# Cross-attention on one core: ScalarE writes the rounded keys to both of their places, instead of one write and a transfer on chip

## What is computed

```python
q = x @ Wq + 2 * (x @ Aq @ Bq)          # 16 x 112 x 1024 -> 32 heads of 32
k = ctx @ Wk + 2 * (ctx @ Ak @ Bk)      # 16 x 375 x 1024 -> 8 heads of 32
v = ctx @ Wv + 2 * (ctx @ Av @ Bv)
scores = einsum('bhqd,bhtd->bhqt', q, k) / sqrt(32)
attn = softmax(scores, axis=-1)
out = x + lora_linear(attn @ v, Wo, Ao, Bo)
```

## Time and profile before

| | us |
|---|---|
| median of 3 runs | 974.63 |
| lowest and highest | 973.23, 975.2 |
| the profiled execution's own time | 971.95 |
| its span, first to last instruction | 969.9 |
| PE busy | 939.5 (97%) |
| VectorE busy | 578.4 (60%) |
| ScalarE busy | 431.7 (45%) |
| GpSimd busy | 320.3 (33%) |

### The profile page before, as it was taken

One profiled execution on the slowest core, in us unless ns is written; L12 is line 12 of the kernel. 1 busy time (PEld: TensorE's weight loads), 2 busy tenths in 40 slices (PEclk: granted clock), 3 DMA queues, 4 the chain that ended last, 5 costly groups with the idle time before them and its releaser, 6 DMA issues.

```text
span 969.9 us, 15636 instructions
## 1 busy us (share of the span) xinstructions
PE 939.5 (97%) x5904; PEld 796.3 (82%) x5904; DVE 578.4 (60%) x1005; ACT 431.7 (45%) x843; POOL 320.3 (33%) x276
## 2 busy tenths in 40 slices
PE   6989999989899999999999999999999989999998
PEld 4879998988878878878888888887887867688886
DVE  5764424246776876776876876876876862343331
ACT  3432313132465665665665665665665644410010
POOL 1300000300244543653553553554454454500000
PEclk9999999999999999999999999999999999999999
DMA  6657597672334534526526526517517364486632
GB/s 197 202 165 197 210 262 268 217 204 66 80 91 108 120 82 117 142 69 152 140 56 165 139 50 172 129 53 174 126 40 184 89 228 125 151 248 207 197 131 87
DMA packets 112794, 141.60 MB, mean 146 GB/s; under 512 B 30688, under 2 KB 90208, under 8 KB 112720
## 3 DMA queue, kind: packets, MB, share of 16 engines
q1 hardware_dynamic: 109552, 129.07, 48.8%
q10 hardware_dynamic: 3168, 11.54, 3.2%
HBM read 95.98 MB, written 38.21 MB: 138 GB/s over the span
## 4 chain that ended last, share of the span: by engine, by line
PE 87%; DVE 5%; DMA 4%; ACT 2%; issue 1%; SPq 1%; POOL 0%; DVEq 0%; POOLq 0%
PE ps L770 13%; PE ps L771 13%; PE ps L772 13%; PE ps L965 9%; PE ps L949 8%; PE ps L980 8%; PE ps L912 5%; PE ps L914 5%; PE ps L916 5%; PE ps L855 4%; PE ps L1016 2%; DMA wo_scratch<-w_sum_qkv 2%; DMA q_scratch<-q_out_lo 1%; PE ps L810 1%; DVE w_sum_qkv L1220 1%
## 5 line engine op out<-in xcount | busy, mean ns | idle before, releaser
L1334 DVE TENSOR_REDUCE maxima<-ps 112x1 f32<-112x375 f32 x512 | 268.4, 542 | 72.1 <-PE ps L965 65.8
L1142 ACT ACTIVATE probs<-ps 125x448 f32<-125x448 f32 x384 | 208.7, 544 | 159.1 <-PE ps L949 157.8
L752 POOL TENSOR_TENSOR prob_sum<-probs 125x448 f32<-125x448 f32 x128 | 148.8, 1178 | 327.3 <-ACT probs L1142 327.0
L965 PE MATMUL ps<-k_stack,q_stack 96*112 96x376 f32 x512 | 177.0, 346 | 5.8 <-DVE maxima L1334 3.0
L758 POOL TENSOR_TENSOR prob_sum<-prob_sum,probs 125x448 f32<-125x448 f32 x128 | 145.4, 1151 | 16.9 <-ACT probs L1142 15.0
L949 PE MATMUL ps<-q_stack,k_stack 97*125 97x448 f32 x384 | 143.6, 374 | 0.0
L912 PE MATMUL ps<-wv_hi,ct_hi 128*125 128x256 f32 x384 | 110.9, 289 | 0.0
L916 PE MATMUL ps<-wv_hi,ct_lo 128*125 128x256 f32 x384 | 108.4, 282 | 0.0
L914 PE MATMUL ps<-wv_lo,ct_hi 128*125 128x256 f32 x384 | 108.2, 282 | 0.0
L1251 DVE TENSOR_TENSOR ct_lo<-ps,ct_hi 128x375 fp32r<-128x375 f32 x128 | 70.2, 548 | 54.7 <-ACT ct_hi L1076 54.7
L965 PEld LDWEIGHTS ps<-k_stack,q_stack 96*112 96x112 f32 x512 | 90.8, 177 | 10.0 <-DVE maxima L1334 5.4
(11 more groups left out here) (85 smaller groups left out, 1463.1 us busy)
## 6 DMA issues: line engine op xcount, KB each, us to landing
ctx_in<-in_ctx_dram SPq DMA_DIRECT2D x16, 1344.0 KB
q_stack<-q_scratch SPq DMA_DIRECT2D x96, 224.0 KB, 4.3
x_in<-in_x_dram SPq DMA_DIRECT2D x8, 896.0 KB, 8.7
q_scratch<-q_out_hi SPq DMA_DIRECT2D x16, 448.0 KB, 3.4
q_scratch<-q_out_lo SPq DMA_DIRECT2D x16, 448.0 KB, 4.2
attn_scratch<-attn SPq DMA_DIRECT2D x32, 224.0 KB, 4.1
attn_rows<-attn_scratch SPq DMA_DIRECT2D x14, 512.0 KB, 5.2
inv_tile<-inv_scratch SPq DMA_DIRECT2D x56, 128.0 KB, 5.5
```

The lines of the kernel that those rows point to most:

```text
L752: pool.tensor_tensor(prob_sum[:, j, :], probs[:, 0, j, :], probs[:, 1, j, :], ALU.add).then_inc(psum_added, 1)
L965: mm = pe.matmul(ps[0:NQ, banks[i % len(banks)], 0:NTE], qst[nxt][0:STK, g, rr * NQ:(rr + 1) * NQ], kst[nxt][0:STK, g, :], start=True, sto ...
L1142: act.activation(probs[:, c, j, :], ps[0:TR, score_bank(i), 0:QH], ACT.Exp, scale=SM).then_inc(exp_done, 1)
L1334: dve.tensor_reduce(maxima[:, h, i:i + 1], ps[0:NQ, banks[i % len(banks)], 0:NT], AX.X, ALU.max).then_inc(max_done, 1)
```

## The change

`k_hi` issues two ScalarE copies per head instead of one: from the same PSUM rows to rows 0 to 31 and to rows 32 to 63 of `k_stack`. The count `k_hi_set` goes up after the second. The transfer `twin_k`, its semaphores `k_in`, and PE's wait for them are gone. SyncE's load of the next context, which stood behind the first transfer of a step, now follows its own wait only.

```diff
@@ sync
-            def twin_k(b, half):
-
-                sp.wait_ge(k_hi_set, NKV * b + (half + 1) * JH)
-                heads = slice(half * JH, (half + 1) * JH)
-                sp.dma_start(kst[b % 2][HD:2 * HD, heads, :].bitcast(F32), kst[b % 2][0:HD, heads, :].bitcast(F32)
-                             ).then_inc(k_in[half][b % 2], 16)
-
...
-                        elif kind == "F0" and i == JH - 1:
-                            twin_k(b + 2, 0)
-                            if "C" in has[h]:
-                                sp.wait_ge(ct_turned, (b + 3) * KC)
-                                load_ctx(b + 3)
-                        elif kind == "F1" and i == JH - 1:
-                            twin_k(b + 2, 1)
+                        elif kind == "F0" and i == JH - 1 and "C" in has[h]:
+                            sp.wait_ge(ct_turned, (b + 3) * KC)
+                            load_ctx(b + 3)
@@ tensor, piece N
                                 pe.wait_ge(q_in[h][nxt], 48 * (pair + (off + 1) // 2 + 1))
-                                pe.wait_ge(k_in[h][nxt], 16 * (pair + (off + 1) // 2 + 1))
                                 pe.wait_ge(k_lo_set, JH * (m + 1))
@@ scalar, k_hi
                 act.wait_ge(k_done, 2 * b + half + 1)
                 at_least(act, st_done, NS * (2 * (b - 2) + half + 1))
-                act.activation(kst[b % 2][0:HD, half * JH + j, :], ps[HD * j:HD * (j + 1), (VA, TURN)[half], 0:NTE],
-                               ACT.Copy).then_inc(k_hi_set, 1)
+                for quad in range(2):
+                    op = act.activation(kst[b % 2][HD * quad:HD * (quad + 1), half * JH + j, :],
+                                        ps[HD * j:HD * (j + 1), (VA, TURN)[half], 0:NTE], ACT.Copy)
+                op.then_inc(k_hi_set, 1)
```

More of the change, by code:

```diff
@@ L323, in xattn_kernel @@
         k_lo_set = sem("k_lo_set")
-        k_in = [[sem(f"k_in{h}{par}") for par in range(2)] for h in range(HALVES)]
         v_done = sem("v_done")
```

## The result

The changed kernel takes 1005.48 us (median of 4 runs, 1004.67 to 1006.53) against 974.91 us: a ratio of 1.0306 with a 95% interval of 1.0286 to 1.0327 (the two medians divided give 1.0314). That is 30.6 us slower; 1007 was forecast, within 996 to 1020. The profiled execution took 1006.53 us, its span is 1004.6 us.

What follows compares the result with a forecast made beforehand. PE was taken to bound the kernel, held by ScalarE's exponentials at P. Steps 28.0, startup 3.2 and clock 1.3 sum to 32.5 us: 1004.5 against the profile, 1007.1 against the median, range 996 to 1020.

Steps and rivals of the forecast that it cites:

- What bounds: PE, busy 939.5 of 969.9 us; ScalarE's exponentials delay P 16 times, 4.1 us in all, with no slack there.
- Removal costs and gains nothing in the steps: Steady steps: removing 32 transfers and SyncE's waits, and the context load up to 6 us earlier, changes nothing.
- 0.49 us per write, 1.97 ahead of the last exponential: Steady step, ScalarE: four added writes delay P by 1.83 to 1.97 us, taken as 1.9.
- VectorE's chain: Steady step behind P: third scores matmul another 0.2 us late, less one ScalarE overlap of 0.1; 2.0 us per step.
- terms (a) to (c): Startup, PE waiting for VectorE: batch 0's third scores matmul +0.6 us, transpose of maxima +0.9, matmul at 254.49 +1.7.
- the clock 1.3: Startup: longer PE idles bring two slow-clock stretches, 1.3 us added, between 0 and 3.4.
- The cheaper second write: Rival, 8%: the second write of a pair costs 0.38 us, stall 1.4 us per step, 22 us in all, 997 us.
- The clock never fell at a P: Judges a rival, 8%: the clock falls at every P, up to 1.7 us more per step, 24 us, 1031 us.
- The faster case: Rival, 4%: the exponential does not release P, writes fit the slack, the startup wait goes: 970.4 us.
- no change: Rival, 4%: the copies are cheap and PE catches up from unseen slack: 974.6 us.
- a sign of overlap: Ahead of P: P waiting under 1.5 us would show the forecast wrong.

Runs made afterwards that it cites:

- e2_no_transfer: The changed kernel without the second write, rows 32 to 63 holding ones, so only the transfers are removed: 971.33 us, ratio 0.9964.
- e6_moved: All 128 second writes, no transfers, but placed behind the last exponential and between the next step's first exponentials; against the kernel before: 975.38 us, ratio 0.9993.
- e1_both: The kernel before with the added ScalarE writes, all transfers and PE's wait for them kept: 1005.82 us, ratio 1.0317.
- e3_half0: The kernel before with the second write for the first key half only, the second half's still by transfer: 998.26 us, ratio 1.0239.
- e5_count_first: The changed kernel's order, but a head's first write releases VectorE and the second write reads the first's result in SBUF: 1006.02 us, ratio 1.0306.
- e7_first_only: The kernel before, with ScalarE writing the second place for batch 0's first half only, in place of that transfer: 972.13 us, ratio 0.996.

## Why the prediction was right, step by step

- **What bounds** was right: PE, held by ScalarE's exponentials at P. e2_no_transfer and e6_moved show the two sides of it.
- **Removal costs and gains nothing in the steps**: right, in e2_no_transfer to 0.03 us in the mean of the periods.
- **0.49 us per write, 1.97 ahead of the last exponential**: 1.94 measured. Of the 0.20 us between exponential and P, 0.15 was slack. I took 1.9 as the step's term, with 1.83 as the bound below; it was 1.79, just outside, as both small errors pointed the same way.
- **VectorE's chain**: forecast 0.2 less one overlap, 0.1 in all; measured 0.15 to 0.17, of which 0.09 at the third scores matmul and the rest at the fourth, which the forecast left out. The overlap of 0.1 us exists (the exponential at 487.88 to the copy at 488.32 is 0.44 for an instruction of 0.54), as I had set against it. The sum per step, 2.0, was 1.96; 14 steps made 27.4 us where I had 28.0.
- **Startup**: terms (a) to (c) made 3.2 us and the clock 1.3, so 4.5; the profile has 5.8. Net of the 0.9 us late start, the third scores matmul of batch 0 came 0.7 us late for a forecast of 0.6. The transpose came 0.3 us late for 0.9 + 0.6: the slow stretch that the kernel before had around 220 us did not come, and gave some back. Then two slow stretches followed. They take 5.1 us from PE's clock against 1.7 before: 3.4 more, my upper bound for a term that I had set at 1.3. The second alone, which was the longer, lies over a stretch that grew by 2.8 us (from 258.38 to the first P at 274.86, where it was 254.49 to 268.14). That the startup's sum still came within 1.3 us is partly luck: up to the transpose it was 1.2 too high, behind it 2.5 too low (5.5 for 1.7 + 1.3). The term that was mis-sized is the clock's.
- **Against the medians** the total of 30.6 leaves 3.2 for everything outside the 27.4 of the steps. Against that, both my terms were a little high (28.0 and 4.5); against the profile the startup was too low (4.5 for 5.8). Two profiled executions can't tell how the startup varies; five kernels that have added writes ahead of or behind P took 56.9 to 64.7 us from first copy to first P. The profiled execution of before is also 2.7 us below the median of the runs that I had; where the others lose that is not known.
- **The rivals.** The cheaper second write did not come: from PSUM the copies of a row keep 0.49 us. The clock never fell at a P in the changed kernel; what I had set against it came true, as part of the delay stands inside the K piece and only 1.34 us ahead of P. The faster case was excluded by e1_both, no change by e1_both, e3_half0 and e5_count_first.
- **The signs.** Steps 38.8 us apart and copies in groups of 4, 2, 2 and 8 came as written. P's waits came smaller, 23.8 us in all for 28, and 1.65 us for about 2; PE's own idle there, 1.34 us, is under the 1.5 that I had named as a sign of overlap, and it was none: I had left out of that sign what PE loses inside the K piece. PE's busy time was 950.5 us where I had written near 940. And the upper end of the range does not follow from its terms: 1013 and half of 24 make 1025, not 1020.

## What to carry to other kernels

An engine that is 45% busy can still have no slack at the one place where the bounding engine waits for it: read the last instructions ahead of that wait before moving work there, and count how many of the added ones would fall ahead of it. If the work must move, give it places of its own in the order, behind the instruction that somebody waits for; here that turned a loss of 30 us into none. And a transfer that nobody waits for is worth nothing when it goes: the one of 32 that was waited for was the only one worth replacing.

## What the runs showed of the hardware that was not expected

**ScalarE's instructions overlapped only where both began at the same partitions.** Four copies of 32x376 from PSUM, whose source moves to other partitions each time, take 1.98 us, 0.50 from start to start, with a gap of 24 ns between them. Four copies of the same shape from SBUF to SBUF, all from the same partitions to the same, take 1.74 us in e7_first_only (the second row above), although each lasts longer (0.50 against 0.48 us): 0.41 from start to start, so 0.09 us of overlap. The Trainium skill's 93 ns ("ScalarE: Activation LUTs", What ACT_TABLE_LOAD costs) is seen in the second group and not in the first. PSUM is not what makes the difference: in the kernel before, the copies of the values out of PSUM, which stay on their partitions, overlap by 0.10 us (16 pairs), and so does an exponential with the copy of a half's first head behind it, where source and destination both start at partition 0 (14 times), but not with that of the third or fourth head (28 times). In the changed kernel's pairs the source stays and only the destination moves; there the gap is 12 ns, in all 128. So moving either was enough to end the overlap, and the second write of a pair was not cheaper. Why is not known.

**The length of an idle stretch alone does not tell whether the clock falls.** The idle of 2.04 us ahead of the transposed maxima kept 2.4 GHz in the kernel before and in e6_moved (granted 1.00 in 246:250); in e2_no_transfer the same 2.04 us (0.58 in 246:250) and in e7_first_only 2.03 us were followed by 1.2 GHz. The row of e7_first_only's timeline and the stretch around it:

```profile
247.85 0.28 PE L975 MATMUL ps<-ident,maxima 112*16 112x112 f32 x1 [2.03 <-DVE maxima L1344]
```

```profile
246.00:250.00 4.00, 2.15 (x8) 2.15 (x9) 1.70 (x4) 0.25 (x1) 0.00 (x0) 0.75 0.88 246
```

In the changed kernel 2.67 us kept the clock and 2.40 lost it. And in e5_count_first, where PE stands still for some 1.7 us at each of 14 P pieces, the clock fell at one of them, and that step took 40.57 us where the others took 38.9:

```profile
404.00:408.00 4.00, 2.26 (x15) 1.38 (x18) 2.74 (x5) 3.81 (x9) 3.04 (x3) 0.89 0.57 144
408.00:412.00 4.00, 4.00 (x34) 0.95 (x24) 2.27 (x4) 2.90 (x6) 0.28 (x1) 0.69 0.00 0
```

So setting the 1.9 us against the 2.04 that kept the clock and the 2.52 that did not was no sound argument, though its result held: none of the 14 stalls of 1.34 us in the changed kernel cost the clock, nor any of the 28 like them in e1_both and e3_half0, and one of 14 a little longer did.
